# First cross-attention of a four-layer transformer kernel: from turning probabilities to computing the scores a second time with the keys on rows

## The reference

```
kv = concat(ctx, x) @ kv_w + kv_b          # keys and values, 320 per sequence
q  = x @ q_w + q_b
s  = q_h @ k_h.T / 16  (+ a mask on the 64 context keys)
p  = softmax(s)                            # over 320 keys
x1 = x + (p @ v_h, heads joined) @ out_w + out_b
x2 = MLP(rmsnorm(x1)) ...                  # 256 -> 1024 -> 256, gelu
```

## Time and profile before

| what | value |
|---|---|
| median of 3 runs | 963.36 us |
| profiled execution, its own time | 961.79 us |
| its span | 959.7 us |
| PE busy | 893.5 us, 93% of the span |
| PEld, DVE, ACT, POOL busy | 747.5, 608.4, 491.0, 490.2 us |
| chain that ended last | PE 71%, DVE 18% |
| granted TensorE clock, mean | 0.984 |
| first score / last output product of this attention | 24.97 us / issued at 180.83 us |

### The profile page before, as it was taken

How to read it: one execution, slowest core, us unless ns; L and a number is a source line. 1 busy time by engine, 2 the same in 40 slices (tenths; PEclk the granted TensorE clock), 3 DMA queues, 4 the chain that set the end, 5 groups by cost and what they waited for, 6 DMA issues and landing times.

```text
span 959.7 us, 15743 instructions
## 1 busy us (share of the span) xinstructions
PE 893.5 (93%) x5624; PEld 747.5 (78%) x5624; DVE 608.4 (63%) x1344; ACT 491.0 (51%) x1204; POOL 490.2 (51%) x509
## 2 busy tenths in 40 slices
PE   3899987899999999999899898899999999999898
PEld 2688876799976789766798787899975789757788
DVE  4687888325779767798332556325779767798340
ACT  1566655663763346533563443764763347633662
POOL 4657777284544245464295162284544335464383
PEclk8799999999999999999999999999999999999999
DMA  8722311101560015300001100201470014200001
GB/s 274 217 79 72 106 49 39 62 2 50 166 235 1 1 48 166 117 0 1 1 23 38 51 1 1 76 25 45 155 253 0 1 44 154 67 1 1 1 12 34
DMA packets 26594, 64.01 MB, mean 67 GB/s; under 512 B 2964, under 2 KB 15764, under 8 KB 25365
## 3 DMA queue, kind: packets, MB, share of 16 engines
q1 hardware_dynamic: 26516, 63.01, 20.1%
HBM read 57.22 MB, written 5.77 MB: 66 GB/s over the span
## 4 chain that ended last, share of the span: by engine, by line
PE 71%; DVE 18%; issue 4%; POOL 2%; ACT 1%; DMA 1%; SPq 1%; DVEq 0%; POOLq 0%
PE ps L949 7%; PE ps L889 6%; PE ps L848 6%; PE ps L850 6%; PE ps L878 5%; PE ps L925 4%; PE ps L762 4%; PE ps L747 3%; PE ps L692 3%; PE ps L693 3%; PE ps L694 3%; PE ps L673 3%; PE ps L675 3%; PE ps L674 3%; DVE prob L1642 3%
## 5 line engine op out<-in xcount | busy, mean ns | idle before, releaser
L949 PE MATMUL ps<-arena,pT_all 128*128 128x256 f32 x512 | 116.9, 381 | 5.8 <-DVE x L1662 3.7
L949 PEld LDWEIGHTS ps<-arena,pT_all 128*128 128x128 f32 x512 | 96.6, 191 | 32.4 <-issue 15.2
L925 PE MATMUL ps<-arena,hT 128*128 128x512 f32 x256 | 115.5, 594 | 0.0
L524 POOL TENSOR_TENSOR rstd<-var,neg_half 128x1 f32<-128x1 f32 (+1 forms) x56 | 33.9, 605 | 153.1 <-DVE var L1471 153.1
L532 POOL TENSOR_TENSOR arena<-arena,rinv 128x640 f32<-128x640 f32 x64 | 80.4, 1256 | 53.5 <-DVE rinv L1456 53.1
L557 POOL TENSOR_TENSOR prob<-prob,rinv 128x512 f32<-128x512 f32 x32 | 49.5, 1547 | 113.3 <-DVE rinv L1655 113.3
L1179 ACT ACTIVATE arena<-ps,nb 128x320 f32<-128x320 f32 x128 | 66.3, 523 | 65.8 <-DVE nb L1441 65.5
L500 POOL TENSOR_TENSOR vacc<-vacc,vpart 128x256 f32<-128x256 f32 x60 | 44.0, 733 | 98.6 <-ACT vpart L1294 98.4
L1222 ACT ACTIVATE arena_r<-ps,cols 128x256 fp32r<-128x256 f32 x128 | 66.2, 517 | 54.0 <-PE ps L675 53.9
L576 POOL TENSOR_TENSOR arena_r<-arena,arena_r 128x512 fp32r<-128x512 f32 x64 | 83.8, 1330 | 13.2 <-ACT arena L1223 13.2
L673 PE MATMUL ps<-hH,w1H 128*128 128x256 f32 x256 | 75.4, 294 | 11.9 <-DVE prob L1642 5.1
(11 more groups left out here) (159 smaller groups left out, 2351.8 us busy)
## 6 DMA issues: line engine op xcount, KB each, us to landing
ring<-in_heads_dram SPq DMA_DIRECT2D x64, 512.5 KB, 3.4
w<-in_w_dram SPq DMA_DIRECT2D x8, 1024.0 KB, 6.6
first_r<-spare_k SPq DMA_DIRECT2D x24, 160.0 KB
first_q<-spare_q SPq DMA_DIRECT2D x48, 64.0 KB, 2.8
spare_k<-HL SPq DMA_DIRECT2D x8, 320.0 KB, 2.5
spare_q<-HL SPq DMA_DIRECT2D x8, 256.0 KB, 2.2
x<-in_x_dram SPq DMA_DIRECT2D x1, 1024.0 KB, 10.1
lnb<-in_lnb_dram SPq DMA_DIRECT2D x4, 256.0 KB, 6.9
```

The lines of the kernel that those rows point to most:

```text
L925: last = mm(ps[:, SCORES[k][half], :], hT[:, k, d, 0:P], A[:, d, b // 2, cols_of, sl, :].rearrange("p r s k -> p r (s k)"), start=(d == 0) ...
L949: last = mm(ps[:, 6, 0:D], pT[:, k, c, :], VW[:, b, c, :], start=(c == 0), stop=(c == PAIRS - 1))
```

## The change

The loop now goes over 32 pairs instead of 64 tiles. A *half* (h, 8 of them) is four pairs of one sequence. The scores are computed twice:

1. `highest(p, u)`: scores of pair p for 128 queries as before, but each head has its own 64 rows of the array (49 in use), and the result serves only for the maxima (`max0` on DVE). Both u use the same two PSUM banks. After four pairs the 8 columns of maxima are turned on PE (`turn_shift`), scaled by -1 on ACT (`turned_shift`) and sent by SP (`shift0`) into a row beside the queries.
2. `lowered(p, rest)`: 7 steps later (LEAD), the same scores with keys on rows, and the maximum already taken off through that extra row. Two calls: four fp32r products of 128x256 into two banks, then two fp32 products of 64 rows and 64 columns into a third. ACT `exp0` writes the exponentials straight into the layout that `values` wants, so the transposes, `copy0`, the POOL multiplication and the accumulated sums go.
3. `values(k, part)`: for two pairs, 5 key blocks x 4 fp32 products of 32 columns x 256 queries on four column strips. Two strips hold the values, two hold ones (`select`), which give the sums of the probabilities in the same layout. DVE `norm0`, once per half, takes two reciprocals of 64x256 and multiplies.

```diff
@@ constants
+HALVES = 2 * B
+NP = PAIRS * B
+SETS = 4
+LEAD = 7
@@ SP
-            spread0(0, 0)
-            spread0(0, 1)
+            spread0(0)
+            sp.dma_start(kinT[:, :, 1:B, :], t["kinT"][:, :, 1:B, :]).then_inc(in_kin, 16)
+            spread0(1)
+            spread0(2)
+            shift0(0)
+            sp.dma_start(ctxT[:, :, :, :], t["ctxT"]).then_inc(in_w0, 16)
+            sp.dma_start(ow0, t["ow0"]).then_inc(in_w0, 16)
+            sp.dma_start(x[:, :, :], t["x"]).then_inc(in_w0, 16)
+            sp.dma_start(brow[:, :, :], t["brow"]).then_inc(in_w0, 16)
             load_mlp(0)
-            for b in range(1, B):
-                spread0(b, 0)
-                spread0(b, 1)
+            for h in range(1, HALVES):
+                if h + 2 < HALVES:
+                    spread0(h + 2)
+                shift0(h)
@@ PE
+                def highest(p, u):
...
+                    if p > 0 or u > 0:
+                        pe.wait_ge(nb_ready, 2 * p + u)
                     for e in range(2):
+                        at = slice(64 * e, 64 * e + 49)
+                        last = mm(ps[:, e, 0:KEYS0], Q0[at, h % SETS, j, u * P:(u + 1) * P],
+                                  K0(h % SETS)[at, j, :], start=True, stop=True)
+                def lowered(p, rest):
...
+                    if p > 0:
+                        pe.wait_ge(p0_ready, 2 * p if rest else 2 * p - 1)
+                    for c in range(1 if rest else 2):
+                        for e in range(2):
+                            at = slice(64 * e, 64 * e + 50)
...
+                def values(k, part):
...
+                    for c in ((2, 4) if part else (0, 1, 3)):
+                        for w in range(2):
+                            for p in (2 * k, 2 * k + 1):
+                                j = (p + 2 * w) % 4
+                                o = ps[32 * j:32 * j + 32, 5 + h % 2, w * S:(w + 1) * S]
+                                lhs = select[:, (0, 0, 1, 2, 2)[c], :] if w else V0[:, b, c, p % PAIRS, :]
+                                last = mm(o, lhs, PT0(p, c), start=(c == 0), stop=(c == 4))
...
+                for i in range(NP + LEAD + 2):
+                    if i < NP:
+                        highest(i, 0)
+                    if 0 <= p < NP:
+                        lowered(p, False)
+                    if p >= 2:
+                        values(p // 2 - 1, p % 2)
+                    middle(step, b)
+                    if i < NP:
+                        highest(i, 1)
+                    if 0 <= p < NP:
+                        lowered(p, True)
+                    aside(step, b)
@@ ACT
+            def exp0(p, part):
+                act.wait_ge(st_ps, 2 * p + part + 1)
+                if part:
+                    a_(PT0(p, 2), ps[:, 4, 0:S], ACT.Exp, scale=-1.0).then_inc(p0_ready, 1)
+                    return
...
+                a_(PT0(p, 0, 2), ps[:, 2, :], ACT.Exp, scale=-1.0)
+                a_(PT0(p, 3, 2), ps[:, 3, :], ACT.Exp, scale=-1.0).then_inc(p0_ready, 1)
@@ DVE
+            def norm0(h):
...
+                sums = ps[:, 5 + h % 2, S:2 * S]
+                v.reciprocal(crow[0:C, :], sums[C:P, :])
+                link(v.reciprocal(crow[C:P, :], sums[0:C, :]))
+                v.tensor_tensor(oT0[:, b % 2, :, m, :], ps[:, 5 + h % 2, 0:S].rearrange("p (u n) -> p u n", u=2),
+                                crow[:, :].rearrange("p (u n) -> p u n", u=2), ALU.mult).then_inc(norm0_ready, 1)
@@ POOL
-                g.tensor_tensor(w, w, rinv[:, n % 2, 0:2].unsqueeze(2).broadcast_to([P, 2, KEYS0]), ALU.mult)\
-                    .then_inc(w0_pool, 1)
+            for n in range(TILES):
+                add_row(x0, n, "L0_out_b")
+            for j in range(16):
+                split_weights(0, j)
```

More of the change, by code:

```diff
@@ new lines, in shift0 @@
+            def shift0(h):
+                sp.wait_ge(shift_ready, h + 1)
+                for e in range(2):
+                    sp.dma_start(Q0[64 * e + 49:64 * e + 50, h % SETS, :, :].bitcast(F32),
+                                 shift[4 * e:4 * e + 4, h % 2, :].bitcast(F32)).then_inc(in_shift[h % 2], 16)
+            spread0(0)
[3 more added lines that the diff above has]
+            shift0(0)
@@ new lines, in values @@
+                def values(k, part):
+                    h, b = k // 2, k // 4
+                    if not part:
+                        pe.wait_ge(p0_ready, 4 * k + 4)
+                        if k % 4 == 0:
+                            pe.wait_ge(v0_ready, 3 * b + 3)
+                        if k % 2 == 0 and h >= 2:
+                            pe.wait_ge(norm0_ready, h - 1)
+                        if k == 0:
+                            pe.wait_ge(hl_ready, 4)
+                            pe.wait_ge(select_ready, 5)
+                    for c in ((2, 4) if part else (0, 1, 3)):
[6 more added lines that the diff above has]
+                    if part:
+                        last.then_inc(pv0_ps, 1)
@@ L766, in output, with turn_shift @@
+                def turn_shift(h):
+                    pe.wait_ge(nb_ready, 8 * (h + 1))
+                    for u in range(2):
+                        last = nc.tensor.transpose(ps[0:8, 7, u * P:(u + 1) * P],
+                                                   nb0[:, h % 2, u, :, :].rearrange("p e j -> p (e j)"), ident[:, :])
+                    last.then_inc(shift_ps, 1)
                 def output(g):
@@ L769, in output @@
                     pe.wait_ge(o0_ready, 2 * (g // 2 + 1))
-                    bank = 6 if g == TILES - 2 else 7
+                    bank = 5 if g == TILES - 2 else 7
                     for d in range(DH):
@@ L774, in output, with middle @@
                     last.then_inc(o_ps, 1)
+                def middle(step, b):
+                    if step == 3 and b + 1 < B:
+                        pe.wait_ge(hl_ready, 4 * (b + 1) + 2)
+                        values_of(b + 1, 0)
+                        values_of(b + 1, 1)
+                    elif step == 7 and b + 1 < B:
+                        pe.wait_ge(hl_ready, 4 * (b + 1) + 4)
+                        values_of(b + 1, 2)
                 def aside(step, b):
@@ L1143, in copy @@
                 return a_(out, in_, ACT.Identity, bias=bias)
+            act.wait_ge(pool_set, 1)
+            for s in range(2):
+                width = (3840, 1280)[s]
+                for e in range(2):
+                    row = slice(64 * e + 49, 64 * e + 50)
+                    k = first_r[row, 0:3840] if s == 0 else arena_r[row, 13056:14336]
+                    act.dma_start(k.bitcast(F32).rearrange("p (k n) -> p k n", n=P),
+                                  ones[0:1, :].unsqueeze(1).broadcast_to([1, width // P, P])).then_inc(row_set, 16)
+            for e in range(2):
+                act.dma_start(first_q[64 * e + 48:64 * e + 49, :].bitcast(F32).rearrange("p (k n) -> p k n", n=P),
+                              ones[0:1, :].unsqueeze(1).broadcast_to([1, 32, P])).then_inc(row_set, 16)
+            a_(mx2[:, 0, 0:1], ones[:, 0:1], ACT.Exp)
             act.wait_ge(in_vec, 64)
@@ L1152, in base0 @@
                 if b >= 1:
[L1154 removed]
+                    act.wait_ge(hl_out[w], 32 * (2 * (b - 1) + m + 1))
                 if t == 1:
```

452 lines of the change are left out of this document (231 added, 221 removed).

## The result

| | before | after |
|---|---|---|
| median, same chip | 962.78 us (4 runs) | 991.13 us (4 runs, 987.89 to 994.96) |
| ratio | | 1.0295, 95% interval 1.0263 to 1.0328 |
| profiled execution, its span | 961.79, 959.7 us | 991.33, 989.5 us |
| mean granted clock | 0.984 | 0.955 |
| first score | 24.97 us | 21.27 us |

The change costs 28 us, and all of it lies in this attention: its last products are issued 31.4 us later, and what is behind them takes as long as before (959.7 - 180.8 = 778.9 us against 777.3).

A forecast was written before the change was run, and what follows sets the result against it. PE's order of work was taken to bound the kernel. Fill, loop, drain and tail summed to +6.9 us, the clock added 8, together +15: 978 us for the median, range 956 to 1003.

The forecast's parts named there:

- the likeliest case: Whole kernel: slower, 978 us for the median, own range 968 to 990 us, chance 0.53.
- stand of PE behind `norm0`: In the loop, PE stands 3.6 us once a half, waiting for a maximum behind DVE's reciprocals.
- first score to first `lowered`: Fill: seven pairs of maxima alone at 3.6 us, 25.2 us, plus 2 us for the low clock.
- to the last `highest`: Loop: five pairs at 3.5 us, twenty at 4.4, 7 us waiting for the second shift, plus 6 for the clock.
- wait for a shift: At pair 4, PE waits 7 us (0 to 9) for the second shift, delayed behind 4.5 MB of loads.
- drain, to the last `values`: Last seven pairs, without `highest`, at 3.5 us each: 24.5 us.
- tail: After the drain: last `norm0` 4.4 us, ACT's bias 0.5, outputs 2.3.
- PE's work falls: In the loop, PE's work per half of four pairs falls by 2.8 us, from 17.1 to 14.3.
- The rivals on layouts, 995 and 1002: Row halves not side by side, 995 us, chance 0.15; four strips run two at a time, 1002 us, chance 0.12.
- 988 for the second part of `lowered` alone: Part of the row-halves rival: both heads' products, writing to one bank, run serially; 988 us.
- the clock's term: PE granted half speed after stands behind `norm0`, 6 us (0 to 12), and in the fill, 2 us; together 8.
- The rival of a cheap `norm0`: Reciprocals at a copy's rate, `norm0` 1.2 us, stands gone; faster, 954 us, chance 0.14.

The follow-up runs named there:

- Experiments 9: The kernel of experiment 7 with one table for logarithm and exponential, loaded once at the start; 959.66 us, ratio 0.998.
- experiment 12: Logarithm division with one table, unread PE products in the fill, and the 4.5 MB of loads in four parts behind shifts of halves 1 to 4; 951.17 us, ratio 0.9875.
- experiment 2: The changed kernel with copies in place of the two reciprocals of `norm0`, so without the division; 962.74 us, ratio 1.0015.
- (3): The changed kernel with the reciprocals of halves 0 to 4 in four 64x128 pieces behind successive maxima; 976.75 us, ratio 1.0146.
- experiment 4: The changed kernel with extra PE products that nobody reads, in the fill and in the stands; 984.36 us, ratio 1.0225.
- experiment 1: The changed kernel with all eight gelus of the first sequence behind ScalarE's last exponential; 990.53 us, ratio 1.0285.
- experiment 7: The changed kernel with gelus as in experiment 1 and the division as exp(-ln(sum)) on ScalarE, no reciprocal on DVE; 975.31 us, ratio 1.015.
- experiment 10: The changed kernel with unread products in fill and stands, and the big loads issued from ScalarE's queue behind the first shift; 981.53 us, ratio 1.0198.

## Why the prediction was right, and where its terms were off

The time, 991, lies in the range, 1 us above the likeliest case's own (968 to 990), and the cause is the one forecast. Point by point, in the profiled executions:

| step | predicted | measured |
|---|---|---|
| reciprocal 64x256 | 1.95 us | 1.76, 1.75 |
| stand of PE behind `norm0` | 3.6 | 2.66 |
| first score | 20.3 | 21.3 |
| first score to first `lowered` | 25.2 + 2 clock | 30.8 |
| to the last `highest` | 112.5 + 6 clock | 120.0 |
| of this, wait for a shift | 7 | 0 |
| drain, to the last `values` | 24.5 | 35.0 |
| tail | 7.2 | 7.1 |
| end | 189.7 + 8 | 214.2 |

- **PE's work falls, the four strips and row halves side by side: right.** The rivals on layouts, 995 and 1002, and 988 for the second part of `lowered` alone, are out by the rows above; that 991 lies near them is chance. The Trainium skill, page "TensorEngine Tiling (Array Packing)", "Gotcha 1: PSUM Pressure", would have had the products at 92.42 one after the other; the trace does not agree. Experiments 9 and 12 show the work itself: from first `lowered` to last `highest`, 25 pairs, 94.6 and 91.7 us, 3.8 and 3.7 a pair. The prediction had 14.3 / 4 = 3.6 for PE's work; before it was 4.3. A change of the array's layout, put at 0.12 us, adds 0.09 to 0.21 us in experiment 12: from the last start of `values` to `highest` 0.31 us, where products of `values` follow each other by 0.22, and from `highest`, 0.13 long, to the fp32 part of `lowered` 0.34.
- **`norm0` turns the gain into a loss: right, and shown three times.** Without the reciprocals the loss is gone (experiment 2), with them in pieces half of it (3), and with the division on ScalarE the loss is gone and the result kept (9). There are five stands, as the sum of the loop had it (20 pairs at 4.4); the clock's term and the price of the cheap `norm0` counted seven. The rival of a cheap `norm0` gave 954 for that case; it measured 962.7, 9 us more. That rival left the drain as it was, and the drain took 32.4 us here, 8 more than predicted.
- **The clock: right in kind, too small.** PE was granted half speed through most of the fill and in stretches of the loop, 0.56 from 21.3 to 51.6 us and 0.63 from 140 to 172. I had 8 us. In the fill alone a fuller clock brings 6 (46.1 against 52.1 in experiment 4). In the loop it hides in the table: without the shift's 7 us the prediction had 111.5 us for that row, and 120.0 were measured.
- **The wait for the second shift: 7 predicted, 0 measured.** The mechanism was right, as experiment 4 shows with 8.1 us. I had put PE's need for it at 59.5 us by a fill at 25.2; the fill at half clock took 30.8 and covered it. Two terms of the sum were thus one: one could not be had without losing the other.
- **The drain, 10.5 us too small: the largest miss.** Some 5 of it goes with ScalarE's changes between exponential and gelu (experiment 1, 29.6): PE waits 3.1 us there instead of 5.9, at a clock of 0.99 instead of 0.90. The other 5 lies in PE's own work: in experiment 12's drain, all at full clock, PE is busy 26.7 us and waits 2.8, where the prediction had 21.0 of work and 3.5 of waiting. 176 records of `values` lie in the drain, 20 a pair, so nine pairs' worth and not seven, some 2 us; what the rest is I have not split further.

The misses are +1.0, +3.6, +1.5, +10.5 and -0.1, in all 16.5; which is 13 in the medians. The sum came as near as it did because the wait that did not occur (7 us) made up for clock that did: that part is luck.

## What to carry to other kernels

When two engines hand one buffer back and forth, whatever stands between two of their steps is on the path, however idle its engine: price it there, move it to a third engine or cut it. Look at what a slow stage hides before pricing its faults one by one: here a slow fill hid a late transfer, and repairing the fill alone brought 7 us of 28 (experiment 4), and the wait then showed. And load big blocks in parts between the small transfers that somebody waits for.

## What the runs showed of the hardware

- A reciprocal on DVE costs 6.9 ns a column (64x256 from PSUM, 1.76 us) where a copy costs 1.7 (0.43 us). The Trainium skill, page "VectorE: DVE Perf Modes", section "First, the fixed hardware budget", has it as an iterative divide with a repeat count of 8; no run here shows how it divides; the ratio is 4.1 against a copy, and it takes 7.4 ns a column in pieces of 128.
- A change of ScalarE's table costs 1.28 us each time (experiment 7), and the logarithm and the exponential can share one (experiment 9).
- Two row halves of the array and four column strips each run side by side in full, the halves into one bank too (starts 0.01 and 0.02 us apart, the next 0.22 to 0.27 us later).
- A block of 4.5 MB holds up what is issued behind it: SP stood 8.3 us for the landing of the writes behind it in its own queue (experiment 4), and a 4 KB transfer from another queue landed after 11.1 us instead of 2.4 (experiment 10).
